# In the softmax loop of a graph kernel, each group of gathers waits until the group before it has landed

## The chip, the cores and the metric

The kernel runs on one core of one Trainium2 chip. The metric is device time in microseconds (us); less is better. The core has five engines with their own instruction queues: PE (matrix products), DVE (vector), ACT (scalar, activation), POOL (GpSimd) and SP (here only for starting DMAs). They meet through semaphores. All DMAs of the core run on the same 16 DMA engines.

## The reference

Two graph layers over 6250 nodes of 128 features and 100,000 edges, each followed by a residual sum and a layer norm.

```
# layer 0
f    = (e @ fc_w.T).reshape(-1, 4, 128)
feat = sum_heads(leaky_relu(attn[rel] * f, 0.2))
x    = layernorm(x + segment_sum(x[src] + feat, dst))
# layer 1, edges (src, dst)
h    = x @ W.T + b
s1, s2 = h @ a1_w + a1_b, h @ a2_w + a2_b
e    = leaky_relu(s1[src] + s2[dst], 0.01)
att  = softmax of e over the edges of each src
x    = layernorm(x + segment_sum(att * h[dst], src))
```

## The kernel before

The kernel has three stages. The first goes through the edges of layer 0 in 196 groups of 512 edges and also sorts the edges by blocks of 122 source nodes into a table in DRAM. A short middle stage computes h and writes its rows to DRAM (`h_rows`, 130 floats a row: the 128 features, a column of ones and s2). The third stage, called the softmax loop here, is the one that the change touches. It goes through the sorted edges in groups of `GE` = 512, four (`TG`) times 128. The number of groups is found on the chip; with this input it is 208. `G1_LEAST` is 200, the count that no input can be under. A running maximum for every source node allows the softmax in one pass: each group rescales what was summed before.

Each engine runs the same sequence of groups g in its own instruction stream, with buffers that return every few groups:

- POOL, `group1` (L539 to L547): waits for the indices of group g (`i1_ready`) and, from group 8 on, until group g - 8 has been used up (`o_done`); then issues four indirect DMAs, each of which gathers 128 rows of 520 bytes from `h_rows` into buffer g mod 8 (`hg`). Each raises the semaphore `g_in[g mod 8]` by 16 when it has landed, 64 for a group. POOL does nothing else in the loop.
- SP, `sources` (L455): loads the local source numbers of a group, spread over all partitions (128 KB), four groups ahead, once DVE has used the buffer (`mT_ready`).
- ACT: `idx` (L668) copies the indices of group g + 5 for POOL; `penalty` (L682), `probs` (L695), `scale` (L701, multiplies the gathered rows by their weights, in place), `decays` (L689).
- PE, in each step g: `rows(g + 2)` (L885, needs the gathered rows of group g + 2, by `g_in`, and the finished maximum of group g), `back(g)` (L896), `attend(g - 3)` (L906, the weighted sum of the rows of group g - 3; it raises `o_done`).
- DVE, in each step g: `update(g - 5)` (L1273, needs attend of that group), `maximum(g)` (L1306, needs rows of that group), then small steps for the running maximum up to L1342, `members(g + 2)` (L1263), `spread(g - 2)` (L1348).

The order on each engine is written out by hand. Most groups are unrolled in Python; the last ones run in a loop on the chip (`Fori`), since their number is only known there, a round for 8 groups (`S1`), on DVE for 4 (`D1`). On PE, ACT and DVE a last set of 8 groups follows the loop.

Of the kernel before, what the change touches and what calls it, by code (L numbers as in the profile page):

```python
# [27 lines left out]
TG = 4  # L28
# [6 lines left out]
G1_LEAST = 8 * -(-G0 // 8)  # L35
# [5 lines left out]
S1 = 8  # L41
LAG = 5
AHEAD = 5
D1 = 4
# [7 lines left out]
RSLOTS = 4  # L52
# [9 lines left out]
def build(nc, x, x_t, e, src_pg, dst_pg, dst_g, rel_g, fcT, attn, WT, Wn, b, a1, a1b, a2, a2b, out):  # L62
    with ExitStack() as ctx:
# [6 lines left out]
        def sems(name, n):  # L70
            return [sem(f"{name}{i}") for i in range(n)]
# [149 lines left out]
        before = accT[0:NS, 2 * GE:2 * GE + T0]  # L221
# [125 lines left out]
        g_in = sems("g_in", S1)  # L347
# [26 lines left out]
        def pass_count(eng):  # L374
            eng.wait_ge(s_passes, 1)
            return eng.value_load(passes[0:1, 0:1], min_val=1, max_val=MAX_PASSES)


        def group_count(eng):
            eng.wait_ge(s_count, 1)  # L380
            return eng.value_load(more_groups[0:1, 0:1], min_val=0, max_val=G1 - G1_LEAST)

        def meet(eng, p):


            eng.sem_inc(pass_end, 1)
            eng.wait_ge(pass_go, p + 1)
            eng.sem_inc(meet_turn, 1)
# [5 lines left out]
        def _(sp):  # L394
# [59 lines left out]
            def sources(g, k, lead):  # L454
                if not lead:  # L455
                    sp.wait_ge(mT_ready, g - RSLOTS + 1)
                sp.dma_start(loc_row[:, k % RSLOTS, :],
                             loc_dram[bass.ds(g, 1), :].to_broadcast([P, GE])).then_inc(loc_in[k % RSLOTS], 16)
# [11 lines left out]
                sources(k, k, True)  # L470

            more = group_count(sp)
            for g in range(RSLOTS, G1_LEAST):
                sources(g, g % S1, False)
            with sp.Fori(G1_LEAST, sp.snap(more + (G1_LEAST - S1 + 1)), S1) as i:
                for k in range(S1):
                    sources(i + k, k, False)

# [12 lines left out]
        @block.gpsimd  # L491
        def _(pool):
            pool.iota(iota_i[:, :], pattern=[[1, 2 * P]], base=0, channel_multiplier=0).then_inc(s_iota, 1)
            pool.iota(iota_ci[:, :], pattern=[[0, 1]], base=0, channel_multiplier=1).then_inc(s_iota, 1)
            pool.wait_ge(s_filled, 16)

            def group(g, k, lead):
                pool.wait_ge(pk_ready, g + 1)
                if not lead:
                    pool.wait_ge(x_added, g - SLOTS + 1)  # L500
                pool.sem_inc(pool_turn, 1)
                for u in range(TG):
                    pool.indirect_dma_start(xg[:, k, u, 0:P], None, x[:, :], bass.IndirectOffsetOnAxis(  # L503
                        ap=pks[:, k, u:u + 1], axis=0)).then_inc(xg_in[k], 16)

            def scatter(g, k, lead):

                pool.wait_ge(r_copied, 2 * g + 2)
                if k:
                    pool.wait_ge(sc_in[k - 1], PASS_SC * p + 16 + (g - k) * 4)  # L510
                elif not lead:
                    pool.wait_ge(sc_in[SLOTS - 1], PASS_SC * p + g * 4)
                pool.sem_inc(pool_turn, 1)
                pool.indirect_dma_start(table[:, :], bass.IndirectOffsetOnAxis(ap=ridx[:, k:k + 1], axis=0),  # L514
                                        runs[:, k, :], None).then_inc(sc_in[k], 16)

            with pool.Fori(0, pass_count(pool)) as p:
                for k in range(SLOTS):
                    group(k, k, True)
                    if k >= RLAG:  # L520
                        scatter(k - RLAG, k - RLAG, True)
                for g in range(SLOTS, G0):
                    group(g, g % SLOTS, False)
                    scatter(g - RLAG, (g - RLAG) % SLOTS, False)
                for j in range(RLAG, 0, -1):
                    scatter(G0 - j, SLOTS - j, False)
                for k in range(SLOTS):
                    pool.wait_ge(xg_in[k], PASS_IN * (p + 1))
                meet(pool, p)


            pool.memset(o_all, 0.0).then_inc(o_zero, 1)
            for c in range(HCHUNKS):
                pool.wait_ge(n_hb, HC * (c + 1))
                pool.dma_start(h_dram.rearrange("(b p) k -> p b k", p=BN)[PMAIN:BN, HC * c:HC * (c + 1), :],
                               h_sb[PMAIN:BN, HC * c:HC * (c + 1), 0:HROW]).then_inc(h_small, 16)
            pool.wait_ge(h_out, 16 * HCHUNKS)
            pool.wait_ge(h_small, 16 * HCHUNKS)

            def group1(g, k, lead):  # L540
                pool.wait_ge(i1_ready, g + 1)
                if not lead:
                    pool.wait_ge(o_done, g - S1 + 1)
                pool.sem_inc(pool_turn, 1)
                for u in range(TG):
                    pool.indirect_dma_start(hg[k][:, u, :], None, h_dram[:, :], bass.IndirectOffsetOnAxis(  # L546
                        ap=idx1[:, k, u:u + 1], axis=0)).then_inc(g_in[k], 16)  # L547

            more = group_count(pool)
            for k in range(S1):  # L550
                group1(k, k, True)
            for g in range(S1, G1_LEAST):
                group1(g, g % S1, False)
            with pool.Fori(G1_LEAST, pool.snap(more + (G1_LEAST - S1 + 1)), S1) as i:
                for k in range(S1):
                    group1(i + k, k, False)

            for q0, q1 in CHUNKS:
                full = min(q1, NS - 1)
                pool.wait_ge(fin_act, q1 // 2)  # L560
                pool.wait_ge(fin_dve, q1 // 2)
                pool.dma_start(out[q0 * BN:full * BN, :].rearrange("(b p) k -> p b k", p=BN)[PMAIN:BN, :, :],
                               xn[PMAIN:BN, q0:full, :]).then_inc(out_small, 16)
            pool.wait_ge(out_small, 16 * len(CHUNKS))
# [3 lines left out]
        def _(act):  # L568
# [96 lines left out]
            def idx(g, k, lead):  # L665
                if not lead:
                    act.wait_ge(g_in[k], 16 * TG + (g - k - S1) * 8)
                nc.scalar.activation(idx1[:, k, :], sd[:, bass.ds(g * TG, TG)], ACT.Copy).then_inc(i1_ready, 1)  # L668
# [35 lines left out]
            def step1(g, k, lead, ahead=True):  # L704
                if ahead:
                    penalty(g + 2, (k + 2) % S1, lead and k < S1 - 2)
                if not (lead and k < 2):
                    probs(g - 2, (k - 2) % S1, lead)
                    scale(g - 2, (k - 2) % S1, lead)
                if not (lead and k == 0):  # L710
                    decays(g - 1, (k - 1) % S1, lead)

            more = group_count(act)
# [8 lines left out]
            for k in range(S1):  # L722
                idx(k + AHEAD, (k + AHEAD) % S1, k < S1 - AHEAD)
                block_s1(k + AHEAD, (k + AHEAD) % S1, k < S1 - AHEAD)
                step1(k, k, True)
            for g in range(S1, G1_LEAST - S1):
                idx(g + AHEAD, (g + AHEAD) % S1, False)
                block_s1(g + AHEAD, (g + AHEAD) % S1, False)
                step1(g, g % S1, False)
            with act.Fori(G1_LEAST - S1, act.snap(more + (G1_LEAST - 2 * S1 + 1)), S1) as i:  # L730
                for k in range(S1):
                    idx(i + k + AHEAD, (k + AHEAD) % S1, False)
                    block_s1(i + k + AHEAD, (k + AHEAD) % S1, False)
                    step1(i + k, k, False)
# [22 lines left out]
        def _(pe):  # L757
# [159 lines left out]
            more = group_count(pe)  # L917
# [2 lines left out]
            rows(1, 1, True)  # L920
            for k in range(S1):
                step1(k, k, True)
            for g in range(S1, G1_LEAST - S1):
                step1(g, g % S1, False)
            with pe.Fori(G1_LEAST - S1, pe.snap(more + (G1_LEAST - 2 * S1 + 1)), S1) as i:
                for k in range(S1):
                    step1(i + k, k, False)
            for k in range(S1):
# [6 lines left out]
        def _(dve):  # L935
# [441 lines left out]
            more = group_count(dve)  # L1377
# [2 lines left out]
            members(1, 1, True)  # L1380
            for k in range(S1):
                step1(k, k, True, k, k - 2)
            for g in range(S1, G1_LEAST - S1):
                step1(g, g % S1, False, g % S1, (g - 2) % S1)
            with dve.Fori(G1_LEAST - S1, dve.snap(more + (G1_LEAST - 2 * S1 + D1 + 1)), D1) as i:
                half = dve.snap(i & (S1 - D1))
                other = dve.snap(S1 - 2 - half)
                for k in range(D1):
                    step1(i + k, k, False, half + k, half + (k - 2) if k >= 2 else other + k)
# [79 lines left out]
```

## Time and profile before

| | us |
|---|---|
| median of 3 runs | 2995.32 (2993.55 to 2998.19) |
| the profiled execution | 2996.43 |
| its span, first to last instruction | 2994.6 |
| POOL busy in the span | 2000.6 (67%) |
| PE busy | 2386.8 (80%) |
| DVE busy | 2350.5 (78%) |
| gathers of the softmax loop, POOL busy | 785.0, 832 instructions |
| first of them starts, last starts | 1666.7, 2922.1 |

The span is what lies between the first and the last instruction of the profiled execution. Busy time of POOL in a DMA instruction is the issue of the DMA, not its transfer. The releaser that the profile puts down for an idle time is inferred: "issue" is time in which the engine waited for nothing that the profile shows, "remote" a release by something that it does not name. Mean DMA rate is 82 GB/s.

### The profile page before, as it was taken

Reading aid. Unit: us, or ns where it says so; the run is one execution under the profiler, and the core shown is the slowest. Engines: PE = TensorE matmul, PEld = TensorE weight load, DVE = VectorE, ACT = ScalarE, POOL = GpSimd, SP = SyncE. Lnnn points to the kernel's source line nnn. Section 1 sums busy time; section 2 is a strip of 40 time slices with the busy share of each in tenths; the row PEclk is TensorE's granted clock in tenths of the full one; section 3 lists DMA queues with packets and bytes.
Section 4 is the critical chain, followed back from the end, with each engine's and each line's share of the span. In section 5 each row is a group of like instructions: output and inputs, shape, how many; then the busy total and the mean of one; then the engine's idle time right before and its main releaser. Section 6 shows DMA issues by size and latency. Waiting matters only on the chain. (4 is left out here: it accounts for less than half of the span.)

```text
span 2994.6 us, 44539 instructions
## 1 busy us (share of the span) xinstructions
PE 2386.8 (80%) x11705; PEld 1541.4 (51%) x11705; DVE 2350.5 (78%) x5910; ACT 1525.4 (51%) x4524; POOL 2000.6 (67%) x1839
## 2 busy tenths in 40 slices
PE   5899999999999999999997366666666666666662
PEld 2355555555555555555555355555555555555551
DVE  8899999999999999999999455555554555555557
ACT  0366666666666666666665334343343433443433
POOL 0388788778887888888785566666666666666660
PEclk9999999999999999999999665566655666666665
DMA  2233333333333333333332323332232222333322
GB/s 87 67 98 99 95 97 98 99 99 96 97 97 99 98 97 96 96 99 99 99 95 63 79 67 69 65 69 66 65 68 66 68 66 66 69 67 67 66 61 47
DMA packets 156606, 244.12 MB, mean 82 GB/s; under 512 B 40837, under 2 KB 84399, under 8 KB 156227
## 3 DMA queue, kind: packets, MB, share of 16 engines
q0 software_dynamic: 58624, 108.72, 16.7%
q1 hardware_dynamic: 97730, 132.55, 15.3%
q8 instruction: 97, 1.59, 0.2%
q14 instruction: 155, 1.26, 0.1%
HBM read 231.99 MB, written 9.12 MB: 81 GB/s over the span
## 5 line engine op out<-in xcount | busy, mean ns | idle before, releaser
L503 POOL DMA_INDIRECT room<-in_x,pks x784 | 1013.5, 1293 | 351.8 <-issue 238.3
L546 POOL DMA_INDIRECT room<-h_rows,idx x832 | 785.0, 943 | 476.6 <-issue 457.6
L798 PE MATMUL FP<-fc_sb,room 128*128 128x512 f32 x1568 | 834.5, 613 | 4.5 <-DMA room<-in_e 4.5
L597 ACT ACTIVATE w_sb<-WP 128x512 f32<-128x512 f32 x784 | 468.1, 597 | 502.6 <-PE WP L807 306.0
L885 PE MATMUL FP<-ident,room 128*128 128x128 f32 x1664 | 385.8, 405 | 359.2 <-DMA room<-h_rows,idx 224.8
L807 PE MATMUL WP<-at_p,rel_oh 100*128 100x512 bf16 x2352 | 637.7, 379 | 1.7 <-issue 1.7
L885 PEld LDWEIGHTS FP<-ident,room 128*128 128x128 f32 x1664 | 332.4, 297 | 410.6 <-DMA room<-h_rows,idx 255.2
L682 ACT ACTIVATE accT<-accT,neg_big 128x512 f32<-128x512 bf16 x208 | 150.0, 721 | 762.6 <-DVE accT L1263 417.1
L807 PEld LDWEIGHTS WP<-at_p,rel_oh 100*128 100x128 bf16 x2352 | 228.3, 97 | 546.9 <-issue 452.4
L1111 DVE TENSOR_TENSOR z<-FP,w_sb 128x1024 f32<-128x1024 f32 x392 | 479.9, 1224 | 20.8 <-issue 12.3
L1118 DVE SCALAR_TENSOR_TENSOR y<-z 128x2048 f32<-128x2048 f32 x196 | 447.9, 2285 | 0.0
L798 PEld LDWEIGHTS FP<-fc_sb,room 128*128 128x128 f32 x1568 | 267.6, 190 | 70.5 <-DMA room<-in_e 4.7
L701 ACT ACTIVATE room<-room,pr 128x129 f32<-128x129 f32 x832 | 266.6, 392 | 6.8
L1126 DVE TENSOR_TENSOR hs<-y 128x1024 f32<-128x1024 f32 x196 | 238.4, 1216 | 0.0
L604 ACT ACTIVATE boh<-arena,rank_pay 128x52 f32<-128x52 bf16 x784 | 237.2, 375 | 0.0
L514 POOL DMA_INDIRECT sorted_edges<-runs,ridx x196 | 184.1, 939 | 64.9 <-issue 60.8
L817 PEld LDWEIGHTS AP<-doh,room 128*128 128x128 f32 x1568 | 206.3, 192 | 35.2 <-DVE room L1142 6.8
L1273 DVE SCALAR_TENSOR_TENSOR arena<-arena,decay,FP 128x129 f32 x104 | 36.0, 346 | 214.6 <-remote 131.1
L817 PE MATMUL AP<-doh,room 128*128 128x64 f32 x1568 | 197.4, 269 | 6.6 <-DVE accT L1102 4.4
L1273 DVE SCALAR_TENSOR_TENSOR arena<-arena,decay,AP 128x129 f32 x104 | 35.9, 346 | 204.0 <-remote 142.8
L1306 DVE CUSTOM_DVE_ANT_0 hs<-accT,FP 128x512 f32<-128x512 f32 x208 | 141.8, 682 | 29.4 <-issue 21.8
L1263 DVE TENSOR_TENSOR accT<-z,WP 128x512 bf16<-128x512 bf16 x208 | 141.5, 681 | 0.7 <-DVE room L1256 0.7
(222 smaller groups left out, 3071.2 us busy)
## 6 DMA issues: line engine op xcount, KB each, us to landing
room<-in_e SPq DMA_DIRECT2D x196, 256.0 KB
rel_sb<-in_rel_g SPq DMA_DIRECT2D x196, 200.0 KB
z<-sorted_sources SPq DMA_DIRECT2D x208, 128.0 KB
room<-h_rows,idx POOLq DMA_INDIRECT x832
room<-in_x,pks POOLq DMA_INDIRECT x784
sorted_edges<-runs,ridx POOLq DMA_INDIRECT x196
accT<-in_x_t SPq DMA_DIRECT2D x1, 3125.0 KB, 9.8
h_rows<-arena SPq DMA_DIRECT2D x13, 227.5 KB, 2.8
```

What stands on the lines that cost most here:

```text
L503: pool.indirect_dma_start(xg[:, k, u, 0:P], None, x[:, :], bass.IndirectOffsetOnAxis(ap=pks[:, k, u:u + 1], axis=0)).then_inc(xg_in[k], 16)
L546: pool.indirect_dma_start(hg[k][:, u, :], None, h_dram[:, :], bass.IndirectOffsetOnAxis(ap=idx1[:, k, u:u + 1], axis=0)).then_inc(g_in[k], 16)
L597: nc.scalar.activation(w_sb[:, u // 2, u % 2, :], WP[u % 2][:, :], ACT.Copy).then_inc(w_copied, 1)
L604: ins = nc.scalar.activation(boh[:, k % 2, u, :], onehot[:, :, bass.ds(g * TG + u, 1)].rearrange("p b o -> p (b o)"), ACT.Identity, bias=0 ...
L701: nc.scalar.activation(hg[k][:, u, 0:P + 1], hg[k][:, u, 0:P + 1], ACT.Identity, bias=0.0, scale=pr[:, k % 2, u:u + 1]).then_inc(h_scaled, 1)
L798: mm = pe.matmul(FP[u // 2][:, u % 2, :], e_sb[:, k, u, :], fc_sb[:, :], start=True, stop=True)
L807: mm = pe.matmul(WP[u % 2][:, :], rel_oh[:, k % 2, u * P:(u + 1) * P], at_p[:, j, :], start=(j == 0), stop=(j == 2))
L817: mm = pe.matmul(AP_[:, 0:W], msg[:, k % 2, u, :], doh[:, k % 2, u, :], start=(u == 0), stop=(u == TG - 1))
L885: mm = pe.matmul(rows_of(k)[:, u * P:(u + 1) * P], hg[k][:, u, P + 1:P + 2].to_broadcast([P, P]), ident[:, :], start=True, stop=True)
L1111: v.tensor_tensor(z[:, h, :, :], FP[h][:, :, :], w_sb[:, h, :, :], ALU.mult).then_inc(z_done, 1)
L1118: v.scalar_tensor_tensor(y[:, :, :, :], z[:, :, :, :], SLOPE0, z[:, :, :, :], ALU.mult, ALU.max).then_inc(y_done, 1)
L1126: v.tensor_tensor(hs[:, :, :], y_all[:, :, 0:D4 // 2], y_all[:, :, D4 // 2:D4], ALU.add).then_inc(hs_done, 1)
```

## The change

In `group1` on POOL, before the four gathers of group g are issued, POOL now also waits for `g_in` of group g - 1 to reach the count at which all four gathers of that group have landed (groups 1 and up). The second part of the change moves the border between unrolled groups and the loop on the chip: on SP, POOL, ACT, PE and DVE eight groups fewer are unrolled and the loop starts eight groups earlier. The groups and their work stay the same.

```
@@ sync: sources
-            for g in range(RSLOTS, G1_LEAST):
+            for g in range(RSLOTS, G1_LEAST - S1):
                 sources(g, g % S1, False)
-            with sp.Fori(G1_LEAST, sp.snap(more + (G1_LEAST - S1 + 1)), S1) as i:
+            with sp.Fori(G1_LEAST - S1, sp.snap(more + (G1_LEAST - S1 + 1)), S1) as i:
...
@@ gpsimd: group1
                 pool.wait_ge(i1_ready, g + 1)
                 if not lead:
                     pool.wait_ge(o_done, g - S1 + 1)
+                if k or not lead:
+                    before = (k - 1) % S1
+                    pool.wait_ge(g_in[before], 16 * TG + (g - 1 - before) * 8)
                 pool.sem_inc(pool_turn, 1)
                 for u in range(TG):
                     pool.indirect_dma_start(hg[k][:, u, :], None, h_dram[:, :], bass.IndirectOffsetOnAxis(
...
-            for g in range(S1, G1_LEAST):
+            for g in range(S1, G1_LEAST - S1):
                 group1(g, g % S1, False)
-            with pool.Fori(G1_LEAST, pool.snap(more + (G1_LEAST - S1 + 1)), S1) as i:
+            with pool.Fori(G1_LEAST - S1, pool.snap(more + (G1_LEAST - S1 + 1)), S1) as i:
...
@@ scalar, tensor and vector alike
-            for g in range(S1, G1_LEAST - S1):
+            for g in range(S1, G1_LEAST - 2 * S1):
...
-            with act.Fori(G1_LEAST - S1, act.snap(more + (G1_LEAST - 2 * S1 + 1)), S1) as i:
+            with act.Fori(G1_LEAST - 2 * S1, act.snap(more + (G1_LEAST - 2 * S1 + 1)), S1) as i:
```

## Rows read from the trace of the kernel before

**Rows 1.** The page: POOL's busy time, its slices (tenths), and its line of gathers.

```profile
PE 2386.8 (80%) x11705; PEld 1541.4 (51%) x11705; DVE 2350.5 (78%) x5910; ACT 1525.4 (51%) x4524; POOL 2000.6 (67%) x1839
...
POOL 0388788778887888888785566666666666666660
...
L546 POOL DMA_INDIRECT room<-h_rows,idx x832 | 785.0, 943 | 476.6 <-issue 457.6
```

**Rows 2.** Stretches (from:to, length, busy and instructions by engine, granted clock, DMA, GB/s).

```profile
1666.67:2923.01 1256.34, 782.13 (x4092) 701.03 (x4092) 674.75 (x3485) 488.05 (x1833) 784.95 (x832) 0.61 0.30 66
1800.00:2800.00 1000.00, 635.78 (x3316) 568.75 (x3315) 542.05 (x2813) 393.59 (x1489) 626.83 (x665) 0.61 0.30 67
2800.00:2900.00 100.00, 61.59 (x329) 55.15 (x330) 56.67 (x278) 40.50 (x153) 61.12 (x65) 0.64 0.32 66
2923.01:2994.60 71.59, 12.63 (x68) 11.94 (x68) 51.72 (x263) 21.67 (x64) 4.03 (x8) 0.57 0.22 47
```

**Rows 3.** Waits, 1800 to 2800 (us in total, times, longest).

```profile
POOL room L546 <- issue: 372.3, 665, 3.6
...
PE FP L885 <- DMA room<-h_rows,idx: 162.0, 82, 4.2
```

**Rows 4.** Timeline of POOL near 2290 (start, duration, [idle before]).

```profile
2288.32 0.94 POOL L546 DMA_INDIRECT room<-h_rows,idx  x1 [0.30 <-issue]
2289.57 0.94 POOL L546 DMA_INDIRECT room<-h_rows,idx  x1 [0.31 <-issue]
...
2293.32 0.94 POOL L546 DMA_INDIRECT room<-h_rows,idx  x1 [0.30 <-issue]
...
2302.52 0.94 POOL L546 DMA_INDIRECT room<-h_rows,idx  x1 [3.27 <-issue]
```

**Rows 5.** Timeline of PE in the same stretch.

```profile
2290.85 2.08 PE L885 MATMUL FP<-ident,room 128*128 128x128 f32 x8 [1.66 <-DMA room<-h_rows,idx]
...
2292.87 1.77 PE L906 MATMUL FP<-room,z 128*128 128x129 f32 x8
2296.21 1.05 PE L885 MATMUL FP<-ident,room 128*128 128x128 f32 x7 [1.56 <-DMA room<-h_rows,idx]
```

**Rows 6.** DMA activity, tenths in slices of 0.1 us: 2335 to 2339, 1610 to 1614.

```profile
DMA  0000000049910100000000000000012222222222
...
DMA  0000000000000020000000000000000000000000
```

**Rows 7.** Timeline of POOL: end of the first stage, and the softmax loop's start.

```profile
1609.91 0.90 POOL L514 DMA_INDIRECT sorted_edges<-runs,ridx  x1 [1.94 <-issue]
1612.76 2.80 POOL L514 DMA_INDIRECT sorted_edges<-runs,ridx  x1 [1.95 <-DMA sorted_edges<-runs,ridx]
...
1717.52 0.94 POOL L546 DMA_INDIRECT room<-h_rows,idx  x1 [11.04 <-PE AP L906]
```

**Rows 8.** Timeline of PE, POOL and DVE, 2327 to 2339.

```profile
2327.82 1.14 PE L906 MATMUL FP<-room,hs 128*128 128x129 f32 x8
...
2334.25 0.94 POOL L546 DMA_INDIRECT room<-h_rows,idx  x1 [0.30 <-issue]
...
2337.84 0.35 DVE L1273 SCALAR_TENSOR_TENSOR arena<-arena,decay,FP 128x129 f32 x1 [3.19 <-remote]
2338.46 0.94 POOL L546 DMA_INDIRECT room<-h_rows,idx  x1 [3.27 <-issue]
```

**Rows 9.** Timeline of POOL and PE: a landing that PE saw late.

```profile
2240.69 0.94 POOL L546 DMA_INDIRECT room<-h_rows,idx  x1 [0.30 <-issue]
...
2243.98 2.07 PE L885 MATMUL FP<-ident,room 128*128 128x128 f32 x8 [4.01 <-DMA room<-h_rows,idx]
```

**Rows 10.** Timeline of PE and DVE at the end of the softmax loop.

```profile
2926.96 2.07 PE L885 MATMUL FP<-ident,room 128*128 128x128 f32 x8 [4.27 <-DMA room<-h_rows,idx]
...
2928.97 2.07 PE L906 MATMUL AP<-room,w_sb 128*128 128x129 f32 x8
...
2931.64 0.69 DVE L1306 CUSTOM_DVE_ANT_0 hs<-accT,FP 128x512 f32<-128x512 f32 x1
```

More of the change, by code:

```diff
@@ L922, in _ @@
                 step1(k, k, True)
-            for g in range(S1, G1_LEAST - S1):
+            for g in range(S1, G1_LEAST - 2 * S1):
                 step1(g, g % S1, False)
-            with pe.Fori(G1_LEAST - S1, pe.snap(more + (G1_LEAST - 2 * S1 + 1)), S1) as i:
+            with pe.Fori(G1_LEAST - 2 * S1, pe.snap(more + (G1_LEAST - 2 * S1 + 1)), S1) as i:
                 for k in range(S1):
@@ L1382, in _ @@
                 step1(k, k, True, k, k - 2)
-            for g in range(S1, G1_LEAST - S1):
+            for g in range(S1, G1_LEAST - 2 * S1):
                 step1(g, g % S1, False, g % S1, (g - 2) % S1)
-            with dve.Fori(G1_LEAST - S1, dve.snap(more + (G1_LEAST - 2 * S1 + D1 + 1)), D1) as i:
+            with dve.Fori(G1_LEAST - 2 * S1, dve.snap(more + (G1_LEAST - 2 * S1 + D1 + 1)), D1) as i:
                 half = dve.snap(i & (S1 - D1))
```

## The prediction

> **What bounds the kernel now.** Read the page first [rows 1]: POOL is busy 67% of the span, and its line L546, the gathers of the softmax loop, is 832 instructions of 943 ns, four for each of 208 groups. The slices show POOL at 5 or 6 tenths through that loop: nothing there is saturated. The table of stretches [rows 2] gives the part at stake: from the first gather (1666.67) to the end of the last (2923.01) are 1256.34 us, 6.04 a group, and 71.59 us follow. In 1800 to 2800, which holds 665 gathers or 166 groups, a group costs DVE 542.05/166 = 3.26 us, PE 3.82 and ACT 2.37. All three could go faster than 6.04.
>
> The waits of that stretch [rows 3] say who holds whom. PE waits 162.0 us in 82 cases for gathered rows, and POOL idles 372.3 us before 665 gathers. The timeline of POOL [rows 4] splits this: inside a group the idle time is 0.30, so a group runs from 2289.57 to 2293.32 + 0.94 = 4.69 us; a group may follow the one before it after 0.31, or after 3.27. On the mean 372.3 - 665 x 0.30 = 172.8 us are left, 1.04 a group, on top of the 0.30. So POOL's cycle is 4.69 + 1.34 = 6.03. POOL is the pace maker: 5.0 of it is its issue, and the 1.04 is the wait for a free buffer (o_done). PE consumes a group right behind its landing [rows 4, 5]: groups whose issue ended at 2289.26 and 2294.26 have their row products start at 2290.85 and 2296.21.
>
> **The change: what the wait costs.** It puts one wait before each group but the first, for the four gathers of the group before. Nothing of POOL's issue can then lie beside the flight of the last gather: a cycle is 4.69 plus the time from the end of a group's last issue to the first issue of the next. No group start of before shows this wait, so neighbours must bound it.
>
> (a) PE waits for the same semaphores and starts 1.59 us after the end of the issue (2288.32 + 0.94 to 2290.85), 1.95 in the next case [rows 4, 5]. (b) The packets: for the group whose issue ends at 2335.19 [rows 8] the last DMA activity of the gather lies at 2336.3 to 2336.4, 1.2 us after the end [rows 6]. PE thus needs some 0.4 us from the last packet. (c) POOL's own wait for a landing is in the trace too, between the last scatters of the first stage: 1609.91 + 0.90 to 1612.76 is 1.95 [rows 7]. Those are small (the last packet 0.7 us after the end, [rows 6]), so POOL needs 1.25 us from the last packet, more than PE. (d) The same slowness shows at 2337.84, where DVE and POOL seem to be let go together and POOL's instruction starts 0.62 later [rows 8].
>
> So the pause is 1.2 + 1.25 = 2.45 by (b) and (c), or 1.59 + 0.62 = 2.2 by (a) and (d). I take 2.40, nearer the first, since its POOL wait has the same form (older waits, the landing, a semaphore step, an indirect DMA). The ends are 1.59 (POOL as quick as PE) and 2.35 + 0.62 = 3.0 (a landing that PE saw late: 2240.69 + 0.94 to 2243.98 [rows 9]).
>
> The cycle becomes 4.69 + 2.40 = 7.09 in place of 6.03. Over the stretch: 207 x 7.09 + 4.69 = 1472 us against 1256: +216 us.
>
> **What is hidden.** The old waits (i1_ready, o_done) stand before the new one. Gather g needs the attend product of group g - 8, which PE does right after the row products of g - 3. Counted from the end of issue of g - 3 that is over at 1.59 + 2.02 + 2.07 = 5.7 us (2290.85 to 2292.87 [rows 5], 2.07 for an attend [rows 10]), while g itself starts 2 x 7.09 + 2.40 = 16.6 us after it. Today a release comes as late as 9.5 us behind the product (product over at 2328.96, POOL at 2338.46 [rows 8]); 5.7 + 9.5 is still under 16.6, so the 1.04 of today goes. If that cover fails it costs up to 1.04 x 207 = 215 us. DVE's 3.26, PE's 3.82 and ACT's 2.37 fit in 7.09 with more room than in 6.03, so gaps that they win are worth nothing. PE's granted clock, 0.61 in the loop [rows 2], mostly its lower level of 1.2 GHz, can move either way without effect, as PE is not late. Behind a waiting gather on POOL's queue stand only later gathers and, after the loop, the output stores, which wait for the end anyway. SP's loads of source rows go by mT_ready, are not behind POOL, and slow down with DVE's steps.
>
> The loops: POOL, SP, ACT and PE run two rounds of their register loop for one, DVE four for two. Today's loop groups lie mostly in 2800 to 2900 and behind; that slice holds 65 gathers, 6.15 a group [rows 2], 0.1 over the mean. Eight more such groups would be 1 us, and a cycle of 7.09 hides it on every engine.
>
> **Start and end.** Today the first eight groups are issued without a stop and POOL then idles 11.04 us [rows 7]; that lies inside the 1256 and gives way to even cycles. At the end the last landing is seen at 2926.96, 3.95 us after its issue (2923.01), and the maximum of the last group starts at 2931.64 [rows 2, 10]. With 1.6 for the landing some 2 us go. The closing stage stays.
>
> **Sum.** The profiled execution took 2996.43 (span 2994.6 and 1.8 around it): 2996.43 + 216 - 2 = 3210. It lies 1.1 us over the median of the runs, 2995.32, so 3209.
>
> **A rule that speaks against it.** In the trace a gather takes 2.53 us from the start of its issue to PE's reaction (2288.32 to 2290.85). The Trainium skill, DMA: Bandwidth & Descriptors, section "Anatomy of one DMA — SWDGE (gpsimd) path", gives about 2.0 us fixed plus bytes/436e3 for a DMA of this queue; for 128 rows of 520 B that is an estimate of 2.15 us. By that figure the pause would be 2.15 - 0.94 = 1.2, the cycle 5.9 and the time some 2965. The trace has its last packet only at 0.94 + 1.2 = 2.1 us, and every engine reacts later than that.
>
> **Rivals.**
> 1. Not slower. The landing pause takes the place of POOL's pause for buffers: today DVE and PE are let go late while POOL issues [rows 8], and with a stop in each group they would be served at once. This decides where the landing pause is at most 1.34, what POOL idles now; at 1.2 it gives 2996 - 207 x 0.14 - 2 = 2965, at 1.34 it gives 2995. For it: the late releases. Against it: the last packet lies 1.2 after the issue, PE is at 1.59, POOL's own case at 1.95. Chance 0.04, half of it a gain. That the wait is met anyway and changes nothing belongs here: the count asks for all 64 increments of the group before, and POOL now starts 0.31 us behind an issue whose packets take 1.2, so it can hardly be.
> 2. A short pause, as between POOL's scatters, 1.95: cycle 6.64, time 3210 - 207 x 0.45 = 3117. For it: the same engine and the same kind of wait. Against it: a gather moves more rows and its last packet came 0.5 later. Chance 0.12 (3060 to 3165).
> 3. A long pause. A load of source rows (SP) falls on the landing, or the wait for buffers stays in series with it. The first gives 3.0, cycle 7.69: 3210 + 207 x 0.60 = 3334 if it hits each group, 3272 if half; the second 3210 + 215 = 3425. For it: PE's late landings of 2.35 and, at the end, 3.95 [rows 9, 10]. Against it: with even cycles the loads come at a fixed place, and most should miss. Chance 0.16.
>
> **How the numbers follow.** The forecast, 3165 to 3265, has 0.68. About 0.2% (6 us) is what a measurement can tell from no change. Slower is 0.68 + 0.12 + 0.16 = 0.96, same 0.02, faster 0.02. The range, 3110 to 3300, takes rival 2 from its value up and rival 3 to a landing that is late in a little over half of the groups; outside stay 0.04 of rival 1, 0.05 of rival 2 and 0.09 of rival 3.
>
> **What would show it.** After: the first gather of each group has 2.2 to 2.65 us of idle time before it, put down to the DMA of h_rows, the other three 0.30; group starts are 7.1 us apart and even from the first on; POOL's busy time on L546 stays at 785 us; the last group starts near 3134; PE's waits for gathered rows grow in number to nearly one a group; the bytes moved stay. Wrong would be: pauses under 1.35; pauses of two lengths (a collision); a wait on PE's attend before POOL beside the landing; or a group's four issues that take other than 4.69.

## The result, and the profile after

The changed kernel takes 3277.44 us (4 runs, 3277.42 to 3278.42) against 2996.2 us of the kernel before (4 runs): ratio 1.0938, 95% interval 1.0924 to 1.0952, 281 us more. The forecast was 3209 with a range of 3110 to 3300. The time lies in that range, near its upper end, but above the narrower band of 3165 to 3265 that had been given a chance of 0.68. The sign and the mechanism held. The new stop was longer than forecast, mostly because of the data that is gathered.

The page after, answering [rows 1] (after the change L546 is L549, L885 is L888, L906 is L909, L1273 is L1276):

```profile
span 3275.6 us, 44892 instructions
...
PE 2424.2 (74%) x11705; PEld 1588.5 (48%) x11705; DVE 2355.2 (72%) x5910; ACT 1525.6 (47%) x4524; POOL 2000.3 (61%) x1839
...
POOL 0487787877877887788635555555555555454551
...
L549 POOL DMA_INDIRECT room<-h_rows,idx x832 | 784.7, 943 | 757.9 <-DMA room<-h_rows,idx 483.9
...
L888 PE MATMUL FP<-ident,room 128*128 128x128 f32 x1664 | 421.2, 433 | 726.3 <-DMA room<-h_rows,idx 726.3
```

POOL does the same 785 us of issuing, but its idle time before the gathers went from 476.6 to 757.9, and most of it (483.9) is now put down to the landing. All of PE's waits before its row products are put down to it too.

The stretches, answering [rows 2]: the gathers, the middle of the loop, and what follows the last gather.

```profile
1668.12:3205.31 1537.19, 817.95 (x4092) 748.02 (x4092) 682.35 (x3494) 490.27 (x1841) 784.71 (x832) 0.58 0.23 54
1800.00:2800.00 1000.00, 541.28 (x2713) 494.80 (x2713) 444.83 (x2306) 324.10 (x1224) 510.24 (x542) 0.58 0.23 55
3205.31:3275.60 70.29, 11.49 (x68) 10.73 (x68) 49.16 (x252) 19.48 (x57) 4.03 (x8) 0.58 0.22 48
```

The gathers take 1537.19 us where they took 1256.34: this is 280.9 of the 281 us. The end is 1.3 us shorter, the start 1.45 later.

The waits of the middle, answering [rows 3]:

```profile
PE FP L888 <- DMA room<-h_rows,idx: 460.2, 136, 6.1
POOL room L549 <- DMA room<-h_rows,idx: 340.8, 130, 3.5
DVE arena L1276 <- PE AP L909: 271.3, 64, 5.4
DVE arena L1276 <- PE FP L909: 260.5, 65, 6.9
POOL room L549 <- issue: 140.0, 409, 2.8
```

PE waits for a landing 136 times, once for each group of this stretch (542 gathers).

The timeline of POOL and PE, answering [rows 4, 5]:

```profile
2213.64 0.94 POOL L549 DMA_INDIRECT room<-h_rows,idx  x1 [0.30 <-issue]
2216.24 2.07 PE L888 MATMUL FP<-ident,room 128*128 128x128 f32 x8 [3.08 <-DMA room<-h_rows,idx]
2217.06 0.94 POOL L549 DMA_INDIRECT room<-h_rows,idx  x1 [2.48 <-DMA room<-h_rows,idx]
2218.26 2.07 PE L909 MATMUL AP<-room,z 128*128 128x129 f32 x8
2218.31 0.94 POOL L549 DMA_INDIRECT room<-h_rows,idx  x1 [0.30 <-issue]
...
2220.49 0.35 DVE L1276 SCALAR_TENSOR_TENSOR arena<-arena,decay,AP 128x129 f32 x1 [3.90 <-PE AP L909]
2220.80 0.94 POOL L549 DMA_INDIRECT room<-h_rows,idx  x1 [0.30 <-issue]
```

The issue of a group ends at 2214.58. PE begins with it at 2216.24, 1.66 later; POOL goes on at 2217.06, 2.48 later, so 0.82 behind PE on the same semaphore. DVE's update starts 0.16 after the attend product is over (2218.26 + 2.07 to 2220.49); before, the releases came up to 9.5 us late [rows 8]. Over groups 16 to 189 this delay was some 4.8 us on the mean before and has a median of 0.16 now. The old pause of 1.04 us a group is gone.

The pause between groups has a median of 2.47 us (forecast 2.40), but it is not even: 55 of 207 are longer than 2.75. All but two of these are under 3.6, as here behind group 175 (the longest is 4.75, behind group 180):

```profile
2965.44 0.94 POOL L549 DMA_INDIRECT room<-h_rows,idx  x1 [0.30 <-issue]
2969.00 1.23 PE L888 MATMUL FP<-ident,room 128*128 128x128 f32 x4 [4.33 <-DMA room<-h_rows,idx]
2969.82 0.94 POOL L549 DMA_INDIRECT room<-h_rows,idx  x1 [3.43 <-DMA room<-h_rows,idx]
```

And the DMA activity of 2966 to 2970 in tenths, in slices of 0.1 us, to be held against [rows 6]:

```profile
DMA  9222010000394307494830000223233322323322
```

The last gather was issued until 2966.38. Its packets begin 0.6 us later, as usual, but they are strewn over 2967.0 to 2968.1. The load of source numbers follows from 2968.5, when the late part is already over. For the group whose issue ends at 2221.74 (pause 2.42) the same view of 2221 to 2225 is:

```profile
DMA  0595400000000099410000000000000223323333
```

There they come at 2222.4 to 2222.8 and are over in 0.4 us.

### The profile page after: what moved, and what is told of

Same layout as the page of the kernel before. It is cut to its first block and busy times, and to the rows that moved or that the text cites. A ratio compares the mean times of both kernels' runs of the same rounds, so it can differ in the third digit from the quotient of the medians.

```text
span 3275.6 us, 44892 instructions
## 1 busy us (share of the span) xinstructions
PE 2424.2 (74%) x11705; PEld 1588.5 (48%) x11705; DVE 2355.2 (72%) x5910; ACT 1525.6 (47%) x4524; POOL 2000.3 (61%) x1839
## 5 line engine op out<-in xcount | busy, mean ns | idle before, releaser
L549 POOL DMA_INDIRECT room<-h_rows,idx x832 | 784.7, 943 | 757.9 <-DMA room<-h_rows,idx 483.9
L888 PE MATMUL FP<-ident,room 128*128 128x128 f32 x1664 | 421.2, 433 | 726.3 <-DMA room<-h_rows,idx 726.3
L888 PEld LDWEIGHTS FP<-ident,room 128*128 128x128 f32 x1664 | 360.0, 319 | 784.2 <-DMA room<-h_rows,idx 711.5
L1276 DVE SCALAR_TENSOR_TENSOR arena<-arena,decay,AP 128x129 f32 x104 | 36.3, 349 | 427.7 <-PE AP L909 403.8
L1276 DVE SCALAR_TENSOR_TENSOR arena<-arena,decay,FP 128x129 f32 x104 | 36.3, 349 | 403.6 <-PE FP L909 370.5
```

The source lines that it names most:

```text
L888: mm = pe.matmul(rows_of(k)[:, u * P:(u + 1) * P], hg[k][:, u, P + 1:P + 2].to_broadcast([P, P]), ident[:, :], start=True, stop=True)
```

## The experiments

They ran on three chips; whether the chip of the first result is one of them isn't on record. The changed kernel takes nearly the same everywhere (3277 and 3288; its wait alone 3280), the kernel before does not: 2996 in the first result, 2779 on two of the chips, 3012 on the third. A ratio is to be read with the time of the kernel before beside it, and where an expectation counts from 2996, the 2779 of that chip takes its place. A pause below is the idle time of POOL between two groups, and a period the time from one group's start to the next.

**Only the borders of the loops** (the kernel before at 2778.99).

```
# the diff of the change without the three lines of group1
```

> The moved borders between unrolled groups and the loop on the chip, without the new wait. Theory (the wait is the whole loss): as before, 2996 us within 6. Rival (the extra rounds of the register loop, on five engines, have a part in it): up to 2996 + 281 = 3277, the time with both. Eight groups more at the 0.1 us that a loop group costs over the mean would be 1 us.

Measured: 2779.23, ratio 1.0002 (0.9992 to 1.0011). The borders cost nothing. Its trace, the first of a kernel at this level, has no stall on POOL at all:

```profile
L546 POOL DMA_INDIRECT room<-h_rows,idx x832 | 785.8, 944 | 258.4 <-issue 250.2
```

The 258.4 us are 0.31 before each of 832 gathers; all 207 pauses between groups are 0.31, the period is 5.00 us against 6.05 in the kernel before of [rows 2], and DVE's update starts 0.24 us behind the attend product on the mean. Here POOL's issue alone is the bound; 207 x 1.05 = 217 is the difference of the two levels (2996 - 2779). PE's granted clock over 1800 to 2600 is 0.72 here and 0.60 in the kernel before at 2996. A low clock alone does not make the releases late, though, since the changed kernel has 0.58 there and prompt ones.

**A wait for the group before the last.**

```
-                if k or not lead:
-                    before = (k - 1) % S1
-                    pool.wait_ge(g_in[before], 16 * TG + (g - 1 - before) * 8)
+                if k > 1 or not lead:
+                    before = (k - 2) % S1
+                    pool.wait_ge(g_in[before], 16 * TG + (g - 2 - before) * 8)
```

> The new wait, but for the group before last: one whole group may be in flight while the next is issued. Theory (only the flight that POOL must sit out costs): the group before last has landed 1.2 us after its issue, while POOL needs 5.0 for the group between, so the wait is always met and the time is that of before, 2996 within 6. Rival (one more wait instruction on POOL costs something by itself): some 0.1 us a group, 3017.

Measured: 2779.18, ratio 1.0002 (0.9992 to 1.0011), all pauses 0.31. The wait as an instruction is free; what costs is that nothing is issued during the last flight.

**The wait behind the first, or behind the second gather of the group.**

```
-                if k or not lead:
-                    before = (k - 1) % S1
-                    pool.wait_ge(g_in[before], 16 * TG + (g - 1 - before) * 8)
                 pool.sem_inc(pool_turn, 1)
                 for u in range(TG):
+                    if u == 1 and (k or not lead):      # u == 2 in the second kernel
+                        before = (k - 1) % S1
+                        pool.wait_ge(g_in[before], 16 * TG + (g - 1 - before) * 8)
+                        pool.sem_inc(pool_turn, 1)
```

> The new wait stands behind the first gather of a group, so that this gather is issued in the shadow of the landing (0.30 + 0.94 = 1.24 us of it). Cycle by the theory: 7.40 (measured with the wait in front) less 1.24 = 6.16 us, the stretch 207 x 6.16 + 4.7 = 1280 against 1256 before, the time 3020, if the wait for free buffers, 1.04 a group before, no longer comes. Rival (the wait for buffers was hidden by the long pause and comes back): 6.16 + up to 1.04 = 7.2, 3235. Second question: with the wait in front DVE's update followed PE's attend by 0.16 us in each group, before by 4.8 on the mean; a prompt one here speaks for a stop per group as the cause, a late one for the length of the stop.

> The new wait stands behind the second gather of a group: 2.49 us of the landing's 2.66 are covered by issue. Cycle by POOL alone: 7.40 - 2.49 = 4.91, no less than the issue itself, 5.0. Theory A (the wait for buffers comes from late releases, and a short stop in each group makes them prompt): the cycle falls under the 6.03 of before, to 5.0 to 5.5, time 2783 to 2890. Theory B (the late releases come from POOL issuing nearly all the time): the buffers bind again, the cycle is 6.03 and the time 2996.

Measured: 3008.41, ratio 1.0822 (1.0804 to 1.084), and 2810.29, ratio 1.0115 (1.0098 to 1.0132). The periods are 6.105 and 5.144. From the changed kernel's 7.40 a gather beside the flight takes off its 1.25 us: 6.15 for one, and for two 4.90, which is under the issue bound of 5.00, so only the late landings still show. The two theories about the late releases, in both expectations, weren't decided: on this chip the kernel before has no pauses beyond the 0.31, so there was no wait for buffers that could have come back or gone. In the timeline of the first of the two, the wait is the gap before the second gather:

```profile
2305.86 0.94 POOL L550 DMA_INDIRECT room<-h_rows,idx  x1 [0.30 <-issue]
2307.19 2.08 PE L889 MATMUL FP<-ident,room 128*128 128x128 f32 x8 [1.72 <-DMA room<-h_rows,idx]
2307.93 0.95 POOL L550 DMA_INDIRECT room<-h_rows,idx  x1 [1.12 <-DMA room<-h_rows,idx]
```

**The changed kernel again**, on the chip where the kernel before takes 3011.51.

> The changed kernel itself, a second time, on the chip on which the kernel before took 2779 us. Theory: with the wait the pace is 4.69 us of issue plus POOL's pause of 2.66, and neither depends on what made the kernel before slower in its first runs (releases of buffers that came up to 9 us late). So the time stays at 3277 (3265 to 3290), and the ratio to the kernel before, here at 2779, becomes 1.18. Rival: this chip runs both kernels faster by the same factor; then the ratio stays at 1.094 and the time is near 3040.

Measured: 3287.59, ratio 1.0919 (1.0901 to 1.0937); mean pause 2.67, period 7.43. This is not a chip where the kernel before takes 2779, so the run doesn't test the expectation. The next kernel does.

**The wait alone**, borders as before (the kernel before at 2779.43).

> The wait alone, with the borders of the loops as they were before the change. Theory: the borders cost nothing under the landing pause, as they cost nothing in the kernel before (1.0002); the time is that of the changed kernel, 3277 to 3290, its pauses and period the same (2.66, 7.40 to 7.43). Rival: the groups in the loop on the chip are slower by some tenths of a us with the wait in them; then eight looped groups fewer save 2 to 6 us.

Measured: 3280.14, ratio 1.1807 (1.1787 to 1.1826); mean pause 2.68, period 7.43. So the same wait costs 501 us where POOL ran at its issue bound and 281 where it already stalled for 1.04 us a group. The theory that stood with the run before holds: the pace with the wait doesn't depend on what holds the kernel before.

**Without the loads of source numbers** (chip of 3287.59).

```
-            for g in range(RSLOTS, G1_LEAST - S1):
-                sources(g, g % S1, False)
...
-                dve.wait_ge(loc_in[k % RSLOTS], 16 + (g - k % RSLOTS) * (16 // RSLOTS))
+                dve.wait_ge(loc_in[k % RSLOTS], 16)
```

> The changed kernel without SP's loads of source numbers after group 3 (left out: groups 4 and up compare with the numbers of the first four groups, so their sums are of other edges). Theory: the pauses of 2.8 to 3.6 us, 55 of 207, have nothing to do with these loads; they stay, the mean period stays 7.40 and the time is that of the changed kernel within 6 us. Rival (collision with the loads): all pauses become 2.4 to 2.5, the period 7.2, and the time is 207 x 0.19 = 39 us lower.

Measured: 3281.16, 6.4 under the changed kernel on that chip. The long pauses behind the same groups (3, 7, 11 and so on) stay: they are 47 of the 52 over 2.75. The collision with these loads is not what made them. At the start of the loop there is one, though. In the changed kernel the pauses behind groups 1, 2, 4 and 5 are 3.1 to 3.2 us (3.1 to 3.3 on the chip of this run); without the loads they are 2.3 to 2.5. Here is group 1, in the changed kernel and in this one, with the DMA activity of 1680 to 1684 in the first:

```profile
1678.98 0.95 POOL L549 DMA_INDIRECT room<-h_rows,idx  x1 [0.30 <-issue]
1679.15 0.33 SPq L457 DMA_DIRECT2D z<-sorted_sources  x1
1682.37 2.08 PE L888 MATMUL FP<-ident,room 128*128 128x128 f32 x8 [5.78 <-DMA room<-h_rows,idx]
DMA  0231327573462355411000000000000000000000
...
1678.98 0.94 POOL L543 DMA_INDIRECT room<-h_rows,idx  x1 [0.31 <-issue]
1681.47 2.08 PE L882 MATMUL FP<-ident,room 128*128 128x128 f32 x8 [4.88 <-DMA room<-h_rows,idx]
```

**A fifth gather in each group.**

```
                 if k or not lead:
                     before = (k - 1) % S1
+                    pool.wait_ge(x_in[before], 16 + (g - 1 - before) * 2)
                     pool.wait_ge(g_in[before], 16 * TG + (g - 1 - before) * 8)
                 pool.sem_inc(pool_turn, 1)
+                spare = doh[:, :, :, :].rearrange("p s u w -> p (s u w)")[:, k % 2 * HROW:(k % 2 + 1) * HROW]
+                pool.indirect_dma_start(spare, None, h_dram[:, :], bass.IndirectOffsetOnAxis(
+                    ap=idx1[:, k, 0:1], axis=0)).then_inc(x_in[k], 16)
```

> The changed kernel with a fifth gather in each group, ahead of the four, into a tile that nothing reads; POOL waits for its landing too. Its issue costs 0.94 + 0.31, so 208 x 1.25 = 260 us more: 3537, if nothing else changes. Theory (every sixteenth gather lands about 1 us late): the late one is then the last of its group only in one group of 16, so some 13 long pauses instead of 55, mean pause 2.52 instead of 2.66, 29 us less: 3508. Rival (something that happens each fourth group): long pauses stay in about one of four groups, 3537.

Measured: 3552.36, 264.8 over the changed kernel on that chip (forecast of the rival 260). My theory of the sixteenth gather falls. Of 65 long pauses, 46 are behind most of the groups 3, 7, 11 and so on to 175, then 180, 184, 188, 193, 197, 201, 205; the other 19 aren't explained. That list gave the next theory. The input has 52 blocks of 122 nodes (fewer in the last), and the edges of a block fill 4 groups (5 in two cases, 1 in the last block); these are the last groups of the blocks, which are filled up with padding, and every padding place gathers row 0. In the changed kernel's trace 44 of the 55 long pauses are behind such groups, four of the other 11 are the collision at the start, and 7 aren't explained. The pause grows with the number of padding places of the group:

| padding places | 2 | 51 | 87 | 103 | 119 | 144 | 195 | 503 (two groups) |
|---|---|---|---|---|---|---|---|---|
| pause, us | 2.39 | 2.67 | 3.00 | 3.16 | 3.31 | 3.45 | 3.44 | 4.38, 4.75 |

It rises by some 8 ns a place until the last gather (128 places) is full. It stays at 3.45 up to 195 places, and is longer again at 503.

**Padding spread over the table.** The kernel is the changed one with three vector instructions more (the kernel before at 2779.43, on the chip of the wait alone).

```
-            v.tensor_scalar(sd, both, 8, None, ALU.arith_shift_right).then_inc(s_dec, 1)
+            link(v.tensor_scalar(sd, both, 8, None, ALU.arith_shift_right))
+            link(v.tensor_scalar(ssf, both, 0, 48.0, ALU.is_equal, ALU.mult))
+            link(v.tensor_scalar(ssf, ssf, iota_col[:, 0:1], None, ALU.mult))
+            v.tensor_tensor(sd, sd, ssf, ALU.add).then_inc(s_dec, 1)
```

> The changed kernel with other row numbers in the padding places of the edge table: now 48 x partition, where all were row 0. (The last group of each of the 52 node blocks is filled up with padding, which is gathered and then weighted by zero.) In the changed kernel the pause behind a block's last group grows with the number of padding places in it, from 2.4 us at 2 or 3 places to 3.45 at 128 and more, 4.4 to 4.8 at 503, and is 2.47 behind the other groups. Theory (128 packets that read one and the same row of DRAM land late): all pauses become 2.4 to 2.5, mean period 7.2, 207 x 0.19 = 39 us less, less some 3 us for the three added vector instructions: 36 us under wait_only of this call. Rival (the end of a block is late for another reason than the repeated row): pauses as before, time 3 us over wait_only.

Measured: 3241.97 against 3280.14 of the wait alone, 38 us less (forecast 36). The pause behind a block's last group falls from 3.22 to 2.47, behind the others it stays (2.50 and 2.51). Behind the two groups with 503 padding places it is 2.42 and 2.30. Group 175, with 3.43 us above:

```profile
2940.04 0.94 POOL L549 DMA_INDIRECT room<-h_rows,idx  x1 [0.30 <-issue]
2942.56 1.86 PE L888 MATMUL FP<-ident,room 128*128 128x128 f32 x7 [2.99 <-DMA room<-h_rows,idx]
2943.38 0.94 POOL L549 DMA_INDIRECT room<-h_rows,idx  x1 [2.40 <-DMA room<-h_rows,idx]
```

Its DMA activity, 2940 to 2944: the last gather's packets (2941.6 to 2942.0) are over in 0.4 us again.

```profile
DMA  0000978000000000199100000000000000232333
```

**POOL waits for PE's row products** (chip of 3287.59).

```
-                    pool.wait_ge(g_in[before], 16 * TG + (g - 1 - before) * 8)
+                    pool.wait_ge(rows_done, g)
```

> The changed kernel, but POOL waits for PE's row products of the group before (rows_done) in place of its landing. They start 1.82 us after the end of the issue on the mean and take 2.07. Theory (POOL takes 0.6 to 0.8 us longer than the other engines to go on after any semaphore): pause 1.82 + 2.07 + 0.78 = 4.67, period 9.36, time 3277 + 207 x 2.01 = 3693. Rival (only landings reach POOL late; after an engine's semaphore it goes on within 0.16 us as DVE does): pause 4.05, time 3565.

Measured: 3850.31, 157 over the theory and further over the rival. Two terms are in it:

```profile
2300.30 0.94 POOL L548 DMA_INDIRECT room<-h_rows,idx  x1 [0.30 <-issue]
2300.55 10.40 SPq L457 DMA_DIRECT2D z<-sorted_sources  x2
2303.67 2.07 PE L887 MATMUL FP<-ident,room 128*128 128x128 f32 x8 [5.99 <-DMA room<-h_rows,idx]
2306.63 0.94 POOL L548 DMA_INDIRECT room<-h_rows,idx  x1 [5.38 <-PE FP L887]
```

POOL goes on at 2306.63, 0.89 after PE's products are over (2303.67 + 2.07). DVE takes 0.16 after a product of PE, so POOL is as slow after PE's semaphore as after a landing, as the theory had it (0.78). The other term was in neither: PE sees the landing 2.43 us after the issue (2301.24), not 1.66. The median over all groups is 2.48, and it is over 2.2 in 175 of 208. The DMA activity of 2301 to 2305 shows what lies beside it: the load of source numbers now lies on the flight, from 2301.5 on, and the gather's packets come among the load's and end at 2303.2.

```profile
DMA  0000022222699875238441000000000000000000
```

So the collision exists; 0.8 us in each of 207 groups is 166 us, about what the theory lacked. That the load is the cause here is read from the trace and from the first groups of the kernel without loads; this kernel wasn't run without them. In the views of the changed kernel above, at 2224 and 2968, the load begins only after the gather's packets are over, so past the first groups the two seldom meet.

**The wait behind the first gather, again.**

> The kernel with the wait behind the first gather of a group, once more, because the kernel before takes 2779 us on one chip and 2996 or 3012 on two others, while the changed kernel takes 3277 and 3288 on those two. Theory (POOL's pace with a landing wait is the same everywhere, 6.1 us a group here, and only the kernel without a stop in each group falls back to 6.05 where releases come late): time 3005 to 3020 on any chip; if the kernel before is at some 3000 here, the ratio is 1.00 to 1.005 in place of 1.082. Rival (late releases come on top of the landing wait): 3012 + 1.1 x 207 = 3240, ratio near 1.08 again.

Measured: 3007.38, ratio 1.0828 (1.081 to 1.0846), with the kernel before at 2779.43. This chip is again one of the lower level. The time is as forecast on both such chips, but the case that mattered, a chip where the kernel before takes some 3000, wasn't measured.

**The kernel before with its padding spread.**

> The kernel before, with the padding rows spread as in spread_pads and nothing else changed. Theory: without the wait a landing that is 1 us late is hidden, and POOL's stalls have another cause (releases that come late), so the time is that of the kernel before plus 3 us for the added instructions (ratio 1.000 to 1.002), and on a chip where that takes some 3000 POOL's mean pause stays near 1.33. Rival (the late landings set off the late releases): pauses fall toward 0.31 and the time falls by up to 1.02 x 207 = 211 us there.

Measured: 2774.86, ratio 0.9986 (0.9977 to 0.9996). The late landings are hidden where nothing waits for them, as the theory says; instead of costing 3 us it is 4.6 faster. Most of that comes behind the last gather, whose landing nothing hides: PE begins with the last group 1.68 us after its issue, where it is 4.19 in the trace of the moved borders. At this level the profile has no pauses that could go, so the rival wasn't tested. It is the fastest version that was run; the gain is under the 0.2% that I would call a difference.

## Why the prediction was right, and what it mis-sized

**The mechanism.** The cycle is the issue of four gathers plus the flight of the last. The pauses are put down to the landing, the period is 7.40 where 7.09 was forecast, PE waits once a group, POOL's busy time is the same, and one gather ahead of the wait took 1.30 us off the period (1.25 by the theory), a second one 0.96, which brings it near the issue bound.

**The sum.** The term that was mis-sized is the pause of 2.40, taken as one value for all groups. The stretch of gathers was forecast as 1472 us and is 1537, 65 more, and the last group starts at 3200.6 where 3134 was forecast. From the trace:

- The pause was forecast as 2.40, from 1.2 + 1.25 = 2.45 and 1.59 + 0.62 = 2.2. Behind the 155 groups that don't end a block it is 2.485 on the mean: 155 x 0.085 = 13 us. The higher of the two sums was right. Some 3 of the 13 us are the collision at the start.
- Behind the 52 last groups of the blocks it is 3.18: 52 x 0.78 = 40 us. This step was missing. I had a row of it: the 3.95 us at the end [rows 10] belong to group 207, which is all padding, and I read them as a possible collision. The other late landing, [rows 9], is no case of it. It is that of group 94, which has no padding, and there a load of source numbers does lie on the flight, as the reading had it (DMA activity of 2240 to 2244; the issue ends at 2241.63):

```profile
2240.86 0.33 SPq L457 DMA_DIRECT2D z<-sorted_sources  x1
DMA  7241000000499000002323393937712635168364
```

- The issue of a group was 4.69. Nine groups (28, 50, 72 and so on, every 22nd) have 1.67 in place of 0.30 between the first and the second gather: 9 x 1.37 = 12 us. The kernel before had four of them, and a shorter one of 0.92 in group 50. What they are isn't shown. A group's issue of other than 4.69 was on the list of what would be wrong.

13 + 40 + 12 = 65.

**What is hidden.** That the 1.04 of the buffer wait would vanish held (0.16 from product to update). The step counted it against 2996, though, and this belongs to that level alone: at 2779 it isn't there, and the wait costs 501. The step also called it the wait for a free buffer. The profile puts it down to "issue", and no run shows which wait it was.

**The start and the end.** 2 us were to go; it is 1.3 at the end, and the first gather starts 1.45 later.

**The rivals.** The first (not slower) needed a landing pause of at most 1.34; no pause in the changed kernel is under 2.2. The second (1.95) falls with it. The third named 3.0 for a collision. Pauses of that length came, behind a quarter of the groups, but by repeated rows; and pauses of two lengths stood on my list of what would be wrong. The kernel without loads excludes the collision as the cause of the pauses at the ends of the blocks, and the one with spread padding shows the cause. So it is in part luck that the time stayed in the range: its upper part, from 3265 to 3300, was there for the collision, and what filled it was something that the prediction did not have. That upper end was also described too low. By the third rival's own figures 3300 is a landing that is late in 90/124 of the groups, nearly three quarters, not a little over half.

**The rule.** By the figure of the Trainium skill (DMA: Bandwidth & Descriptors, section "Anatomy of one DMA — SWDGE (gpsimd) path") I had the estimate of 2.15 us from the start of the issue. The trace has 0.94 + 1.66 = 2.6 to PE and 0.94 + 2.48 = 3.4 to POOL. The measurement decides: the estimate is near the last packet, not near the next instruction.

## What to carry to other kernels

A wait for one's own last transfer costs a full flight and the engine's own reaction in each round: here 501 us where POOL ran at its issue bound. With one gather issued ahead of the wait it was 229, with two 31, and a wait for the round before cost nothing. When some landings are late at a regular distance, look at what they fetch before looking at what runs beside them: here the position in the data (the last group of a block) gave the cause away. And price an added wait against the bound by issue as well as against the stalls of one trace, since the stalls may not be there on the next chip.

## What the runs showed of the hardware that was not expected

- A gather whose 128 places all read one and the same row in DRAM lands late: the pause is 3.45 us instead of 2.4, and 4.4 to 4.8 where nearly all places of the four gathers do so. With different rows it is 2.47. What in the memory or the DMA engines causes this isn't shown.
- A load of source numbers (128 KB) on the flight of a gather delays the landing: PE begins with group 1 of the changed kernel 2.44 us after the issue, and 1.55 after it in the kernel without the load.
- POOL goes on 0.82 us after PE on the same semaphore, and 0.89 after the end of a product of PE, where DVE takes 0.16.
- The kernel before takes 2779 us on two chips, 3012 on a third, and 2996 in the first result, while kernels with a stop in each group differ by 0.3%. The trace at 2996 has releases that come several us after PE's product, marked "remote" [rows 8], and POOL stalls of 1.04 us a group; those at 2779 have neither (0.31 us on POOL, and a median of 0.16 us from product to update). No trace of the kernel at 3012 was kept. What delays the releases isn't shown, nor whether the chip or something else decides it.
